# Normalised rows transposed by 32x32 blocks on VectorE and brought into channel order through DRAM

## The chip, the cores and the metric

The kernel runs on one core of a Trainium2 chip. The metric is device time in microseconds (us) of one execution, and lower is better. In the text PE is TensorE, DVE is VectorE, ACT is ScalarE, POOL is GpSimd and SP is SyncE, which issues every DMA of this kernel.

## What is computed

The input has 16 sequences of 1024 rows of 256 channels in float32. Each row is layer-normalised, and the normalised row feeds two branches whose results are added to the input:

```python
xn = _layernorm(x, axis=-1)
x = x + _L0_attn_ref(xn, Wqkv, Wout) + _L0_ffn_ref(xn, W1, b1, W2, b2)
# attention: 16 heads of 16 channels, segments of 512 rows; the keys and values are every 8th row of the segment
scores = jnp.einsum('bhspd,bhskd->bhspk', q4, k4)       # 512 queries x 64 keys in each segment and head
c = jnp.max(scores, axis=4, keepdims=True)              # over blocks of 64 queries
w = jnp.exp(scores - c)
out = jnp.einsum('bhsnmk,bhskd->bhsnmd', w, v4) / (jnp.sum(w, axis=-1) + 1e-10)[..., None]
# feed-forward: relu(xn @ W1 + b1) @ W2 + b2, 256 -> 1024 -> 256
```

## The kernel before

The work is cut into 32 segments of 512 rows. A segment's rows lie on 128 partitions, four rows to a partition. The five engines each run their own program, written out by hand, and meet only at semaphores, so the order on each engine is the order of the code. Matrix products are made with float32r operands in three parts: a tensor is split into a high part (a cast, on ACT) and a low part (the difference, on DVE or POOL), and `three_products` (L736 to L742) issues high x high, low x high and high x low.

A step `s` works on three segments at once: the feed-forward and the output product of segment `s` (`ffn`), the attention of segment `s+1` (`attention`), and the projections of segment `s+2` (`norm`), while segment `s+3` is loaded (`load`). All four are on in most steps. `par` is `s % 2`. The keys and values of two segments are projected together, in the steps with `par == 0`, called even steps here; the others are odd steps. A step has eight tiles of the feed-forward: `first_product` makes 128 hidden channels for 512 rows in `h_bank`, `hidden` (ACT) applies ReLU and makes the high part, `hidden_lo` (POOL) the low part, and `second_product` adds into `y_bank`.

What the change touches:

- DVE normalises segment `s+2` early in step `s` (`normalise`, four instructions, `xn` at L622), after the second of the eight `shift_scores`. In an even step `keys_lo` (`xkey_lo`, L598) follows it.
- PE transposes `xn` with eight 128x128 products against an identity into the two PSUM banks `misc` (`transpose_x`, L809), just ahead of the last `first_product` of the step.
- ACT waits for that last `first_product`, since it was still reading the same half of `xt`, and then copies the banks to `xt_hi` (`transposed_hi`, L487). DVE makes `xt_lo` (`transposed_lo`, L651).
- PE makes the queries of segment `s+2` from `xt` (`queries`, the products with `wq`) after `second_product` of tile 6 and the last `scores`.
- SP starts a step with `rden_to_dram`, waits for the two conditions of `load_x`, issues `rden_spread` (reciprocals of the softmax sums, copied to the rows that need them), and then for most of the step `pack`: 24 DMAs that bring keys and queries of pairs of heads to the partitions of the score product. Its last DMA is the output of the step before, `out<-y`.

The order of the eight transposes among the waits of PE is this (L801 to L810):

```python
pe.wait_ge(xn_ready, s + 3)
pe.wait_ge(num_den_ready, past((s + 1) * QUADS))
...
for c in range(DH):
    for t in range(T):
        mm = pe.transpose(misc[c][:, t * P:(t + 1) * P], xn[:, t, c * P:(c + 1) * P], identity[:])
    mm.then_inc(xt_psum, 1)
```

Of the kernel before, what the change touches and what calls it, by code (L numbers as in the profile page):

```python
# [28 lines left out]
P = 128  # L29
# [19 lines left out]
def ln_attention_ffn(nc, x, wq_t, wkv_t, wout_t, w1, b1, w2, b2, out):  # L49
# [18 lines left out]
    with ExitStack() as ctx:  # L68
# [28 lines left out]
        xn = sb("xn", [P, T, D], F32)  # L97
        xn_keys = sb("xn_keys", [P, D], F32)
# [18 lines left out]
        att_part = [sb(f"att_{n}", [P, 2, QUADS, SEG], F32R) for n in ("hi", "lo")]  # L117
# [45 lines left out]
        xn_keys_ready = sem("xn_keys_ready")  # L163
        xkey_psum = sem("xkey_psum")
# [94 lines left out]

        block = ctx.enter_context(nc.Block())  # L260

        @block.sync
        def _(sp):
# [67 lines left out]

            def step(s, par, ffn, attention, norm, load):
                if ffn:
                    rden_to_dram(s)
                if load:

                    sp.wait_ge(x_b2_ready, s + 2)
                    sp.wait_ge(xn_ready, s + 2)
                    load_x(s + 3, 1 - par)
                if load and par == 1:  # L340
                    sp.wait_ge(xn_keys_ready, s + 3)
                    load_keys(s + 3)
# [22 lines left out]
        def _(pool):  # L365
# [32 lines left out]
            def attention_lo(s, quad, par):  # L398
                pool.wait_ge(att_ready, s * QUADS + quad + 1)
                pool.wait_ge(att_hi, s * QUADS + quad + 1)  # L400
                pool.tensor_tensor(att_part[1][:, par, quad], att[:, quad], f32(att_part[0][:, par, quad]),  # L401
# [38 lines left out]
        def _(act):  # L440
# [22 lines left out]
            def attention_hi(s, quad, par):  # L463
                act.wait_ge(att_ready, s * QUADS + quad + 1)
                act.wait_ge(y_psum, past((s - 1) * YB))
                act.copy(att_part[0][:, par, quad], att[:, quad]).then_inc(att_hi, 1)  # L466
# [15 lines left out]
            def transposed_hi(s, par):  # L482

                act.wait_ge(h_psum, past((s + 1) * NH))
                for c in range(DH):
                    act.wait_ge(xt_psum, (s + 2) * DH + c + 1)
                    act.copy(xt[0][:, par, c], misc[c][:]).then_inc(xt_hi, 1)  # L487
# [63 lines left out]
        def _(dve):  # L551
# [65 lines left out]
            def normalise(s, par):  # L617
                dve.wait_ge(stats_ready, s + 1)
                dve.wait_ge(rstd_ready, s + 1)
                dve.wait_ge(xt_psum, past(s * DH))  # L620
# [3 lines left out]
                op.then_inc(xn_ready, 1)  # L624

# [21 lines left out]
            def transposed_lo(s, par):  # L647

                for c in range(DH):
                    dve.wait_ge(xt_hi, (s + 2) * DH + c + 1)  # L650
                    dve.tensor_tensor(xt[1][:, par, c], misc[c][:], f32(xt[0][:, par, c]),  # L651
                                      ALU.subtract).then_inc(xt_lo, 1)
# [82 lines left out]
        def _(pe):  # L735
# [40 lines left out]
            def output_product(s, par):  # L776
                pe.wait_ge(att_hi, (s + 1) * QUADS)
                pe.wait_ge(att_lo, (s + 1) * QUADS)
                for t in range(T):
                    mm = three_products(y_bank[t // 2][:, (t % 2) * D:(t % 2 + 1) * D],  # L780
                                        [([a[:, par, m, t * P:(t + 1) * P] for a in att_part],
# [17 lines left out]
            def transpose_x(s, par):  # L799
# [3 lines left out]
                pe.wait_ge(num_den_ready, past((s + 1) * QUADS))  # L803
                if par == 0 and not (isinstance(s, int) and s == -2):
                    pe.wait_ge(kv_ready, s + 4)
                    pe.wait_ge(k_ready, s + 4)
# [45 lines left out]
            def weighted_values_waits(s, norm):  # L852
# [4 lines left out]
                if norm:  # L857
                    pe.wait_ge(xt_lo, (s + 3) * DH)
# [11 lines left out]
            def step(s, par, ffn, attention, norm, load):  # L870
# [4 lines left out]
                for i in range(LAG, NH):  # L875
# [6 lines left out]
                    if i == NH - 1 and norm:  # L882
# [16 lines left out]
                if attention:  # L899
                    weighted_values_waits(s, norm)  # L900
# [53 lines left out]
```

## Time and profile before

| | |
|---|---|
| median of 3 runs | 1131.28 us (1129.73 to 1131.32) |
| the profiled execution | 1129.96 us, of it a span of 1128.1 us from the first to the last instruction |
| TensorE clock granted, mean | 0.995 |
| busy | PE 97%, DVE 66%, ACT 58%, POOL 55% of the span |
| DMA | 130.57 MB, mean 116 GB/s, packets 45.2% of the time of 16 engines |

A time in the text such as 574.01 is microseconds from the start of the span. The two steps that are read are an even step (about 523.5 to 558.3 us) and the odd step behind it (about 558.3 to 591.5 us). A busy share says how much an engine had to do, not whether the end waited for it; the chain of waits says that. Issue-to-landing times of DMAs run from the start of the issue on SP to the arrival of the last byte.

### The profile page before, as it was taken

The numbers are of one execution on the slowest core, as the hardware profiler recorded it, in microseconds if no ns is written. First come the engines' busy times: TensorE is split into PE (matmuls) and PEld (weight loads), VectorE is DVE, ScalarE is ACT, GpSimd is POOL, SyncE is SP. The second block draws the span as 40 slices with busy tenths as digits, with TensorE's granted clock in tenths as the row PEclk, the third lists the DMA queues.
The fourth block names the chain that finished last, engine by engine and source line by source line (L and its number), as shares of the span: only waits on it lengthen the run. The fifth ranks groups of instructions, "written<-read, shape, count | busy, mean of one in ns | idle before, by whom it ended". The sixth has DMA issues, their size and how long they took to land.

```text
span 1128.1 us, 23167 instructions
## 1 busy us (share of the span) xinstructions
PE 1097.2 (97%) x7457; PEld 944.5 (84%) x7457; DVE 742.9 (66%) x1370; ACT 650.4 (58%) x1078; POOL 620.1 (55%) x488
## 2 busy tenths in 40 slices
PE   5799999999999999999999999999999999999997
PEld 3588988888988888988888988888988888888886
DVE  7787667657666667666667666667676667677540
ACT  4556556555656555555665556565565565555652
POOL 2435555555555555565565556466465565565464
PEclk9999999999999999999999999999999999999999
DMA  5444444344444444445344544444544353544421
GB/s 183 107 119 128 120 125 120 95 123 118 127 122 110 111 112 126 121 115 126 92 126 111 135 108 110 117 120 118 128 103 122 100 134 107 139 102 106 98 77 68
DMA packets 96139, 130.57 MB, mean 116 GB/s; under 512 B 25840, under 2 KB 54128, under 8 KB 96112
## 3 DMA queue, kind: packets, MB, share of 16 engines
q1 hardware_dynamic: 96112, 130.23, 45.2%
q8 instruction: 15, 0.25, 0.1%
q14 instruction: 12, 0.10, 0.0%
HBM read 39.98 MB, written 18.87 MB: 52 GB/s over the span
## 4 chain that ended last, share of the span: by engine, by line
PE 96%; DVE 1%; issue 1%; POOL 1%; SPq 0%; DMA 0%; POOLq 0%; ACT 0%; DVEq 0%
PE y_bank L740 40%; PE h_bank L740 40%; PE s_banks L796 5%; PE misc L866 3%; PE s_banks L866 2%; PE misc L809 2%; PE misc L740 2%; PE misc L834 0%; PE misc L817 0%; PE s_banks L740 0%; DVE w_exp L637 0%; DVE s_max L631 0%; DMA q_pack<-q_hi 0%; DVE xn_keys L592 0%; DVE w_lo L556 0%
## 5 line engine op out<-in xcount | busy, mean ns | idle before, releaser
L389 POOL TENSOR_TENSOR h_lo<-h_full,h_hi 128x512 fp32r<-128x512 f32 x256 | 336.9, 1318 | 454.5 <-ACT h_full L455 450.0
L740 PE MATMUL y_bank<-w_hi,h_hi 128*128 128x256 f32 x1024 | 290.1, 283 | 1.2 <-ACT w_exp L461 1.2
L740 PE MATMUL y_bank<-w_lo,h_hi 128*128 128x256 f32 x1024 | 289.9, 283 | 0.0
L740 PE MATMUL y_bank<-w_hi,h_lo 128*128 128x256 f32 x1024 | 289.5, 283 | 0.0
L461 ACT ACTIVATE w_exp<-w_exp 128x512 f32<-128x512 f32 x256 | 162.6, 636 | 213.7 <-DVE w_exp L637 213.7
L453 ACT ACTIVATE h_hi<-h_bank,b_cols 128x512 fp32r<-128x512 f32 x256 | 175.9, 687 | 122.5 <-PE h_bank L740 117.2
L631 DVE TENSOR_REDUCE s_max<-s_banks 128x8 f32<-128x512 f32 x256 | 175.4, 685 | 64.8 <-PE s_banks L796 63.0
L740 PE MATMUL h_bank<-xt_hi,w_hi 128*128 128x512 f32 x512 | 211.0, 412 | 1.4 <-DVE q_lo L660 1.4
L740 PEld LDWEIGHTS y_bank<-w_hi,h_hi 128*128 128x128 f32 x1024 | 195.1, 191 | 10.7 <-issue 1.4
L740 PEld LDWEIGHTS y_bank<-w_lo,h_hi 128*128 128x128 f32 x1024 | 195.4, 191 | 9.9
L740 PE MATMUL h_bank<-xt_lo,w_hi 128*128 128x512 f32 x512 | 202.4, 395 | 0.0
L740 PE MATMUL h_bank<-xt_hi,w_lo 128*128 128x512 f32 x512 | 201.8, 394 | 0.0
L740 PEld LDWEIGHTS y_bank<-w_hi,h_lo 128*128 128x128 f32 x1024 | 194.6, 190 | 0.0
L637 DVE TENSOR_TENSOR w_exp<-s_banks,s_max 128x512 f32<-128x512 f32 x256 | 177.1, 692 | 11.0
L455 ACT ACTIVATE h_full<-h_bank,b_cols 128x512 f32<-128x512 f32 x256 | 175.1, 684 | 0.0
L707 DVE TENSOR_TENSOR y<-y_bank,x_b 128x512 f32<-128x512 f32 x64 | 44.3, 692 | 146.2 <-PE y_bank L740 146.2
L740 PEld LDWEIGHTS h_bank<-xt_hi,w_hi 128*128 128x128 f32 x512 | 96.6, 189 | 44.1 <-issue 27.8
L740 PEld LDWEIGHTS h_bank<-xt_hi,w_lo 128*128 128x128 f32 x512 | 96.5, 189 | 22.8
L740 PEld LDWEIGHTS h_bank<-xt_lo,w_hi 128*128 128x128 f32 x512 | 97.1, 190 | 14.9
L796 PE MATMUL s_banks<-q_pack,k_pack 96*128 96x512 f32 x256 | 97.3, 401 | 6.5 <-issue 2.3
L651 DVE TENSOR_TENSOR xt_lo<-misc,xt_hi 128x512 fp32r<-128x512 f32 x64 | 41.3, 686 | 86.5 <-ACT xt_hi L487 86.5
L401 POOL TENSOR_TENSOR att_lo<-att,att_hi 128x512 fp32r<-128x512 f32 x64 | 80.9, 1287 | 27.5 <-ACT att_hi L466 27.5
(90 smaller groups left out, 1601.0 us busy)
## 6 DMA issues: line engine op xcount, KB each, us to landing
q_pack<-q_hi SPq DMA_DIRECT2D x256, 128.0 KB, 2.4
x_raw<-x SPq DMA_DIRECT2D x32, 512.0 KB, 3.4
q_pack<-q_lo SPq DMA_DIRECT2D x128, 128.0 KB, 2.4
rden_rows<-rden_dram SPq DMA_DIRECT2D x128, 128.0 KB, 3.5
out<-y SPq DMA_DIRECT2D x32, 512.0 KB, 2.9
k_pack<-k_hi SPq DMA_DIRECT2D x256, 32.0 KB, 1.9
num_den<-num_den SPq DMA_DIRECT2D x32, 256.0 KB, 2.5
k_pack<-k_lo SPq DMA_DIRECT2D x128, 32.0 KB, 1.9
```

The source lines that it names most:

```text
L389: pool.tensor_tensor(h_part[1][:, i % HBUF], h_full[:, i % HBUF], f32(h_part[0][:, i % HBUF]), ALU.subtract).then_inc(h_lo, 1)
L401: pool.tensor_tensor(att_part[1][:, par, quad], att[:, quad], f32(att_part[0][:, par, quad]), ALU.subtract).then_inc(att_lo, 1)
L453: act.activation(h_part[0][:, i % HBUF], h_bank[i % 2][:], ACT.Relu, bias=b1_cols[:, i:i + 1]).then_inc(h_hi, 1)
L455: act.activation(h_full[:, i % HBUF], h_bank[i % 2][:], ACT.Relu, bias=b1_cols[:, i:i + 1]).then_inc(h_ready, 1)
L461: act.activation(w_exp[:, pair], w_exp[:, pair], ACT.Exp).then_inc(w_ready, 1)
L631: dve.tensor_reduce(s_max[:, pair], ps.rearrange("p t n i -> p n t i"), AX.XY, ALU.max).then_inc(max_ready, 1)
L637: dve.tensor_tensor(w_exp[:, pair].rearrange("p (t n i) -> p t n i", t=T, n=NB), ps, top, ALU.subtract).then_inc(s_shifted, 1)
L651: dve.tensor_tensor(xt[1][:, par, c], misc[c][:], f32(xt[0][:, par, c]), ALU.subtract).then_inc(xt_lo, 1)
L707: dve.tensor_tensor(y[:, par, 2 * b:2 * b + 2], y_bank[b][:].rearrange("p (t d) -> p t d", t=2), x_b2[:, par, 2 * b:2 * b + 2], ALU.add).t ...
L740: mm = pe.matmul(ps, stationary[a], moving[b], start=start and c == 0 and n == 0, stop=stop and c == len(pairs) - 1 and n == 2, skip_group ...
L796: pe.matmul(s_bank[n % 2], k_pack[0:PR, pair], q_pack[0:PR, pair], start=True, stop=True).then_inc(s_psum, 1)
L866: mm = pe.matmul(pv_banks[quad][PW * j:PW * (j + 1), a], v[rows, 1 - par, pair], w_exp[rows, pair], start=True, stop=True)
```

## The change

In the steps that have both `ffn` and `norm` (s = 0 to 29, thirty steps), PE no longer transposes `xn`. DVE transposes its 32x32 blocks into a new buffer `z` with one instruction behind `normalise`. SP writes `z` to DRAM in four DMAs, one for each group of 32 partitions, and reads it back in one DMA into `xt_raw`, whose partitions are channels. ACT and DVE make `xt_hi` and `xt_lo` from `xt_raw` in SBUF instead of `misc` in PSUM, with access patterns that put the rows in token order. The first two steps (s = -2 and -1) keep the transposes on PE. Waits on `misc` move accordingly. The attention rows `att_hi` and `att_lo` have one buffer instead of two, and `attention_hi` waits for the output product of the step before (`y_psum` at `s * YB`, it was `(s - 1) * YB`).

```diff
+        z = sb("z", [P, D // PW, T, PW], F32)
+        xt_raw = sb("xt_raw", [P, DH, SEG], F32)
+        xt_dram = nc.dram_tensor("xt_dram", [D // PW, PW, P // PW, P], F32).ap()
...
-        att_part = [sb(f"att_{n}", [P, 2, QUADS, SEG], F32R) for n in ("hi", "lo")]
+        att_part = [sb(f"att_{n}", [P, QUADS, SEG], F32R) for n in ("hi", "lo")]
...
+        def block_order(tile):
+            return tile.rearrange("p (i t n) -> p t i n", i=P // PW, t=T)
+
+        def token_order(tile):
+            return tile.rearrange("p (t i n) -> p t i n", i=P // PW, t=T)
...
+            def blocks_to_dram(s):
+
+                sp.wait_ge(z_ready, s + 1)
+                for i in range(P // PW):
+                    sp.dma_start(xt_dram[:, :, i].rearrange("j c n -> c j n"),
+                                 z[PW * i:PW * (i + 1)].rearrange("c j t n -> c j (t n)")).then_inc(xt_out, 16)
+
+            def transposed_in(s):
+
+                sp.wait_ge(xt_out, (s + 1) * 64)
+                sp.dma_start(xt_raw[:], xt_dram.rearrange("(a j) c i n -> (j c) a (i n)", a=DH)).then_inc(xt_in, 16)
+
             def step(s, par, ffn, attention, norm, load):
+                if ffn and norm:
+                    blocks_to_dram(s)
                 if ffn:
                     rden_to_dram(s)
+                if ffn and norm:
+                    transposed_in(s)
                 if load:
...
             def attention_hi(s, quad, par):
                 act.wait_ge(att_ready, s * QUADS + quad + 1)
-                act.wait_ge(y_psum, past((s - 1) * YB))
+                act.wait_ge(y_psum, past(s * YB))
...
             def transposed_hi(s, par):
 
                 act.wait_ge(h_psum, past((s + 1) * NH))
+                if not (isinstance(s, int) and s < 0):
+                    act.wait_ge(xt_in, (s + 1) * 16)
                 for c in range(DH):
...
+                        act.copy(token_order(xt[0][:, par, c]), block_order(xt_raw[:, c])).then_inc(xt_hi, 1)
...
+            def transpose_blocks(s):
+
+                dve.wait_ge(xn_ready, s + 3)
+                dve.transpose(z[:].rearrange("p j t n -> p t j n"),
+                              xn[:].rearrange("p t (j n) -> p t j n", n=PW)).then_inc(z_ready, 1)
...
+                        dve.tensor_tensor(token_order(xt[1][:, par, c]), block_order(xt_raw[:, c]),
+                                          token_order(f32(xt[0][:, par, c])), ALU.subtract).then_inc(xt_lo, 1)
...
                     if n == 1 and norm:
                         normalise(s + 2, par)
+                    if n == 1 and norm and ffn:
+                        transpose_blocks(s)
                     if n == 1 and keys:
                         keys_lo(s)
...
-                    if i == NH - 1 and norm:
+                    if i == NH - 1 and norm and not ffn:
                         transpose_x(s, par)
```

On PE, between the second product of tile 5 and the last first product of a step, the rows before were these (`L801` and `L755` rows set a register for a wait):

```order
L740 MATMUL y_bank<-w_lo,h_hi 128x256
L740 MATMUL y_bank<-w_hi,h_lo 128x256
L801 REGISTER_ALU
L809 MATMUL misc<-identity,xn 128x128 x8
L755 REGISTER_ALU
L740 MATMUL h_bank<-xt_hi,w_hi 128x512
L740 MATMUL h_bank<-xt_lo,w_hi 128x512
```

and now they are these:

```order
L788 MATMUL y_bank<-w_lo,h_hi 128x256
L788 MATMUL y_bank<-w_hi,h_lo 128x256
L803 REGISTER_ALU
L788 MATMUL h_bank<-xt_hi,w_hi 128x512
L788 MATMUL h_bank<-xt_lo,w_hi 128x512
```

The eight transposes are gone from PE, and nothing stands in their place.

On SP, at the turn from an even to an odd step of the changed program's first steps, the rows before were these:

```order
L303 DMA q_pack<-q_hi 32x2x512
L358 DMA out<-y 128x1024
L322 DMA rden_dram<-rden 128x64
L265 DMA x_raw<-x 128x1024
L269 DMA x_keys<-x 128x256
L328 DMA rden_rows<-rden_dram 32x1x1024 x4
L296 DMA k_pack<-k_hi 32x2x128 x2
```

and now they are these:

```order
L315 DMA q_pack<-q_hi 32x2x512
L386 DMA out<-y 128x1024
L348 DMA xt_dram<-z 32x8x128 x4
L334 DMA rden_dram<-rden 128x64
L354 DMA xt_raw<-xt_dram 128x2x512
L277 DMA x_raw<-x 128x1024
L281 DMA x_keys<-x 128x256
L340 DMA rden_rows<-rden_dram 32x1x1024 x4
L308 DMA k_pack<-k_hi 32x2x128 x2
```

Four writes stand between the output of the step before and the reciprocals, and one read between the reciprocals and the load of the next segment.

On DVE, behind the second `shift_scores` of a step, the rows before were these:

```order
L637 TENSOR_TENSOR w_exp<-s_banks,s_max 128x512
L622 TENSOR_SCALAR xn<-x_raw,mean_var,rstd 128x256 x4
L631 TENSOR_REDUCE s_max<-s_banks 128x8
L637 TENSOR_TENSOR w_exp<-s_banks,s_max 128x512
L631 TENSOR_REDUCE s_max<-s_banks 128x8
```

and now they are these:

```order
L679 TENSOR_TENSOR w_exp<-s_banks,s_max 128x512
L658 TENSOR_SCALAR xn<-x_raw,mean_var,rstd 128x256 x4
L665 STREAM_TRANSPOSE z<-xn 128x4x8x32
L673 TENSOR_REDUCE s_max<-s_banks 128x8
L679 TENSOR_TENSOR w_exp<-s_banks,s_max 128x512
```

One instruction over 1024 elements per partition is added; in an even step `xkey_lo` comes right behind it.

## Rows read from the trace of the kernel before

**Rows 1.** The page, busy time and share of each engine, and granted clock in 40 slices

```profile
PE 1097.2 (97%) x7457; PEld 944.5 (84%) x7457; DVE 742.9 (66%) x1370; ACT 650.4 (58%) x1078; POOL 620.1 (55%) x488
...
PEclk9999999999999999999999999999999999999999
```

**Rows 2.** Chain of waits in order of time, odd step: start us, us, what

```profile
574.01 0.87 PE misc L809 x8
574.89 1.40 PE h_bank L740 x6
```

**Rows 3.** The same chain in the even step

```profile
540.93 0.87 PE misc L809 x8
```

**Rows 4.** Timeline of ACT, DVE and PE: start, us, engine, line; both steps

```profile
576.40 1.07 ACT L487 CAST xt_hi<-misc 128x512 fp32r<-128x512 f32 x2 [2.77 <-PE h_bank L740]
...
577.02 1.29 DVE L651 TENSOR_TENSOR xt_lo<-misc,xt_hi 128x512 fp32r<-128x512 f32 x2 [2.99 <-ACT xt_hi L487]
...
579.46 0.40 PE L740 MATMUL h_bank<-xt_hi,wq_hi 128*128 128x512 f32 x1
...
543.30 1.07 ACT L487 CAST xt_hi<-misc 128x512 fp32r<-128x512 f32 x2 [2.74 <-PE h_bank L740]
...
546.38 0.40 PE L740 MATMUL h_bank<-xt_hi,wq_hi 128*128 128x512 f32 x1
```

**Rows 5.** Timeline of SP's queue at the start of the even and the odd step

```profile
533.60 0.42 SPq L358 DMA_DIRECT2D out<-y  x1
538.48 0.32 SPq L322 DMA_DIRECT2D rden_dram<-rden  x1
539.14 0.35 SPq L265 DMA_DIRECT2D x_raw<-x  x1
...
566.97 0.60 SPq L303 DMA_DIRECT2D q_pack<-q_lo  x1
567.61 0.60 SPq L303 DMA_DIRECT2D q_pack<-q_hi  x1
568.52 0.36 SPq L358 DMA_DIRECT2D out<-y  x1
...
572.60 0.32 SPq L322 DMA_DIRECT2D rden_dram<-rden  x1
573.30 0.34 SPq L265 DMA_DIRECT2D x_raw<-x  x1
```

**Rows 6.** DMA issues: copy, count, KB each, median us from issue to landing

```profile
q_pack<-q_lo SPq DMA_DIRECT2D x128, 128.0 KB, 2.4
...
rden_dram<-rden SPq DMA_DIRECT2D x32, 32.0 KB, 1.4
y<-wkv_t SPq DMA_DIRECT2D x1, 512.0 KB, 5.1
```

**Rows 7.** Landing times of the tiles x_raw and rden_rows, us

```profile
DMA to landing us min/median/max: 3.1/3.4/7.3
...
DMA to landing us min/median/max: 2.5/3.5/4.3
```

**Rows 8.** Groups of instructions by form: count, busy us, mean ns

```profile
L556 DVE TENSOR_TENSOR wkv_lo<-y,wkv_hi 128x1024 fp32r<-128x1024 f32 x1 | 1.2, 1222 | 0.0
```

**Rows 9.** Timeline of DVE and POOL around the normalisation, even step, then odd

```profile
530.51 2.46 POOL L410 TENSOR_TENSOR x_b<-x_raw,b_rows 128x1024 f32<-128x1024 f32 x1
...
530.62 0.41 DVE L598 TENSOR_TENSOR xkey_lo<-misc,xkey_hi 128x256 fp32r<-128x256 f32 x1
...
533.08 0.40 PE L740 MATMUL misc<-wkv_hi,xkey_hi 128*128 128x512 f32 x1
...
561.82 2.36 DVE L622 TENSOR_SCALAR xn<-x_raw,mean_var,rstd 128x256 f32<-128x256 f32 x4
...
562.55 1.47 POOL L389 TENSOR_TENSOR h_lo<-h_full,h_hi 128x512 fp32r<-128x512 f32 x1 [2.83 <-ACT h_full L455]
563.98 2.45 POOL L410 TENSOR_TENSOR x_b<-x_raw,b_rows 128x1024 f32<-128x1024 f32 x1
```

More of the change, by code:

```diff
@@ L163, in ln_attention_ffn @@
         xn_keys_ready = sem("xn_keys_ready")
+        z_ready = sem("z_ready")
+        xt_out = sem("xt_out")
+        xt_in = sem("xt_in")
         xkey_psum = sem("xkey_psum")
@@ L400, in attention_lo @@
                 pool.wait_ge(att_hi, s * QUADS + quad + 1)
-                pool.tensor_tensor(att_part[1][:, par, quad], att[:, quad], f32(att_part[0][:, par, quad]),
+                pool.tensor_tensor(att_part[1][:, quad], att[:, quad], f32(att_part[0][:, quad]),
                                    ALU.subtract).then_inc(att_lo, 1)
@@ L464, in attention_hi @@
                 act.wait_ge(att_ready, s * QUADS + quad + 1)
-                act.wait_ge(y_psum, past((s - 1) * YB))
-                act.copy(att_part[0][:, par, quad], att[:, quad]).then_inc(att_hi, 1)
+                act.wait_ge(y_psum, past(s * YB))
+                act.copy(att_part[0][:, quad], att[:, quad]).then_inc(att_hi, 1)
             def attention_drain(s, quad):
@@ L484, in transposed_hi @@
                 act.wait_ge(h_psum, past((s + 1) * NH))
+                if not (isinstance(s, int) and s < 0):
+                    act.wait_ge(xt_in, (s + 1) * 16)
                 for c in range(DH):
-                    act.wait_ge(xt_psum, (s + 2) * DH + c + 1)
-                    act.copy(xt[0][:, par, c], misc[c][:]).then_inc(xt_hi, 1)
+                    if isinstance(s, int) and s < 0:
+                        act.wait_ge(xt_psum, (s + 2) * DH + c + 1)
+                        act.copy(xt[0][:, par, c], misc[c][:]).then_inc(xt_hi, 1)
+                    else:
+                        act.copy(token_order(xt[0][:, par, c]), block_order(xt_raw[:, c])).then_inc(xt_hi, 1)
             def queries_hi(s, m):
@@ L619, in normalise @@
                 dve.wait_ge(rstd_ready, s + 1)
-                dve.wait_ge(xt_psum, past(s * DH))
+                if isinstance(s, int) and s <= 2:
+                    dve.wait_ge(xt_psum, s * DH)
+                else:
+                    dve.wait_ge(z_ready, s - 2)
                 for t in range(T):
@@ L650, in transposed_lo @@
                     dve.wait_ge(xt_hi, (s + 2) * DH + c + 1)
-                    dve.tensor_tensor(xt[1][:, par, c], misc[c][:], f32(xt[0][:, par, c]),
-                                      ALU.subtract).then_inc(xt_lo, 1)
+                    if isinstance(s, int) and s < 0:
+                        dve.tensor_tensor(xt[1][:, par, c], misc[c][:], f32(xt[0][:, par, c]),
+                                          ALU.subtract).then_inc(xt_lo, 1)
+                    else:
+                        dve.tensor_tensor(token_order(xt[1][:, par, c]), block_order(xt_raw[:, c]),
+                                          token_order(f32(xt[0][:, par, c])), ALU.subtract).then_inc(xt_lo, 1)
             def finish_projections(s, par):
@@ L780, in output_product @@
                     mm = three_products(y_bank[t // 2][:, (t % 2) * D:(t % 2 + 1) * D],
-                                        [([a[:, par, m, t * P:(t + 1) * P] for a in att_part],
+                                        [([a[:, m, t * P:(t + 1) * P] for a in att_part],
                                           [w[:, m, :] for w in wout]) for m in range(DH)],
@@ L801, in transpose_x @@
                 pe.wait_ge(xn_ready, s + 3)
[L803 to L806, printed above, removed]
                 for c in range(DH):
@@ L850, in queries, with weighted_values_waits @@
                                True, True).then_inc(q_psum, 1)
-            def weighted_values_waits(s, norm):
+            def weighted_values_waits(s, par, norm):
                 pe.wait_ge(v_ready, (s + 2) * 2)
                 pe.wait_ge(w_ready, (s + 2) * PAIRS)
-                if norm:
-                    pe.wait_ge(xt_lo, (s + 3) * DH)
+                if norm and isinstance(s, int) and s == -1:
+                    pe.wait_ge(xt_lo, 2 * DH)
+                elif norm and par == 0:
+                    pe.wait_ge(k_ready, s + 4)
             def weighted_values(s, quad, par):
@@ L899, in step @@
                 if attention:
-                    weighted_values_waits(s, norm)
+                    weighted_values_waits(s, par, norm)
                 if ffn:
```

## The prediction, on record before the changed kernel ran

> **What bounds the kernel now.** I read the page first: PE is busy for 97% of the span and its granted clock stays in the top tenth in every slice; DVE, the next, is at 66% [rows 1]. The reader is to see an engine that never rests, beside others with room. Busy time alone proves nothing, so I read the chain of waits next. In both steps it lies on PE all through the transposes, and eight of them stand on it with 0.87 us each time [rows 2, 3]. They finish right where the last first product begins (574.01 + 0.87 = 574.88), so there is no wait around them to fill the gap if they go. Then I read the timeline around the place where the transposed rows are used, and SP's queue, because the new path runs through it.
>
> **The change, part by part.**
>
> *Removed from PE.* Eight transposes in each of thirty steps, on the chain: 30 x 0.87 = 26.1 us. This is the whole gain that is there to be had: 1129.96 - 26.1 = 1103.9 us in the profiled execution.
>
> *When the rows are needed.* ACT starts `xt_hi` when the last first product is through, at 576.40 in the odd step and 543.30 in the even one [rows 4]. Without the transposes both moments come 0.87 us sooner: 575.53 and 542.43. From that start to the end of `xt_lo` it takes 577.02 + 1.29 - 576.40 = 1.91 us [rows 4]. PE wants the result for the queries at 579.46 and 546.38 [rows 4], now at 578.59 and 545.51. So `xt_raw` may land as late as 1.91 us, and some 0.1 us for two semaphores, before these: 576.6 in the odd step, 543.5 in the even.
>
> *The new path through SP.* SP must first finish the packing of the step before. Its last DMA, `out<-y`, starts at 533.60 and 568.52 and takes 0.42 and 0.36 us [rows 5]; then come the four writes of `z`. No row shows such a write. Its issue is nearest to `q_pack`'s, also 32 partitions in several runs, one every 0.64 us [rows 5]. In the odd step they start at 568.95, 569.59, 570.23 and 570.87, in the even one the last starts at 535.98. A write of 128 KB is nearest in size to `q_pack` with 2.4 us from issue to landing; below lies the small write to DRAM, `rden_dram`, with 1.4 [rows 6], above `rden_rows` with up to 4.3 [rows 7]. I take 2.4: the last lands at 573.27 and 538.38. SP meanwhile waits for the reciprocals, whose copy it issues at 572.60 and 538.48 as before, since DVE makes them behind scores that PE sets the time of. So the read goes out at 573.3 in the odd step and 539.1 in the even one, which are the times of `x_raw` before [rows 5].
>
> *The read.* It is 512 KB from DRAM over 128 partitions. `x_raw` has the same size in longer runs: 3.1 at best, median 3.4 us [rows 7]. `wkv_t` has this very form, but was loaded at the start beside other loads: 5.1 us [rows 6]. In the steady steps nothing is in flight ahead of the read but `z`, which it waits for, so I take 3.4: landed at 576.7 and 542.5. The odd step is then late by 576.7 - 576.6 = 0.1 us, and the even one has 1.0 us to spare. Sum: 15 x 0.87 + 15 x (0.87 - 0.1) = 24.6 us.
>
> *Added to DVE.* One block transpose over 1024 elements. No row shows one; the nearest DVE instruction over 1024 elements from and to SBUF takes 1.22 us [rows 8]. A shorter one would change nothing in the sum; upwards no row gives a bound, and I allow twice that, 2.4 us. It delays `xkey_lo`, which ran from 530.62 to 531.03, while its product starts on PE at 533.08 [rows 9]. With 1.22 us it ends at 532.25: hidden. With 2.4 us it ends at 533.43 and costs 0.4 us in 15 even steps, 6 us. The shifts of scores behind it move by the same time, and DVE waits for PE a little later, so they catch up. In the odd step there is no `xkey_lo`. `z` itself is ready near 532 and 565.4, long before SP is free, so DVE's time is not on the new path.
>
> *Moved on SP.* Five DMAs stand ahead of `x_raw` and `rden_rows`. `rden_rows` then lands about 1 us later, and POOL's `att`, `att_hi` and `att_lo` with it; the output product that needs them comes last in the step, behind two tail products of 3 us together, so I cost this at nothing. If that cover were gone, it would cost at most the 1 us, 30 us in all.
>
> *Costed at nothing:* the copies from SBUF instead of PSUM (they are in the 1.91 us; if each of the four took 0.1 us more, 15 odd steps lose 3 us); the single buffer of attention rows (`attention_hi` runs after the queries of its step, the product it now waits for ended a whole step earlier); the waits on `misc`.
>
> *The sum* is 1129.96 - 24.6 = 1105.4 us. The profiled execution is 1.3 us below the median of the runs, so the median should be near 1107.
>
> **The rivals.**
>
> *The round trip through DRAM is longer than its row (ends slower).* Place: the read's landing, ahead of ACT's `xt_hi`. What speaks for it: margins of -0.1 and 1.0 us against two transfers for which there is no row of their own, one behind the other, and an SP queue that is full from `q_lo` to `out<-y`. If queries are late, so are `q_lo`, the next packing and the next writes: nothing is made up. An excess e on the read costs e in the odd step and e - 1.0 in the even one. It decides at 0.1 + e + e - 1.0 = 1.74, that is e = 1.3 us: beyond that the kernel is slower. At the 5.1 us of `wkv_t` e is 1.7: an odd step gains 0.87 - 1.8 = -0.93, an even one 0.87 - 0.7 = 0.17, and 15 pairs lose 11 us: 1143. If the write takes 4.3 us instead, the odd step is 2.0 late and the even one 0.2: loss 0.46 per pair, 1138. Against it: `x_raw`, as large and at the same moment of the step, has a median of 3.4 [rows 7].
>
> *The block transpose waits for POOL.* DVE's fourth `xn` of each step does: four of them take 2.36 us where POOL's `h_lo` runs through their end, 562.55 + 1.47 = 564.02, and they end at 564.18 [rows 9]. POOL's `x_b` comes right behind, until 532.97 in the even step and 566.43 in the odd [rows 9]. If the transpose waits for that, it ends at 534.19 and 567.65. In the even step `xkey_lo` then ends at 534.6 and its product is 1.57 us late: 15 x 1.57 = 23.6 us. In the odd step three shifts of 1.4 us follow, the reciprocals come 1.0 us later, and the read 0.65 us: 10 us. Together 1107 + 34 = 1141. Against it: `xkey_lo`, 0.41 us from 530.62 on, runs beside `x_b` without such a wait [rows 9]. The Trainium skill, "SBUF — State Buffer", in its terms and its account of the engine side, says that DVE and GpSimd share a pair of ports under an exclusive lock, held for a whole instruction, when DVE runs in a two-port mode. By that rule, and if the transpose is such an instruction, this rival's 1141 us comes out; if it reads through one port, my sum stands. The trace agrees with the lock for `xn` and cannot show it for the transpose.
>
> *Part of the gain is eaten.* Excesses of 0.5 to 1.2 us on the new path, or a transpose of 2.4 us: 15 x 0.5 = 8 to 15 x 1.2 + 15 x 0.2 = 21 us less, so 1115 to 1128.
>
> **How the numbers follow.** The forecast (1104 to 1114) has 0.48; the gain partly eaten (1114 to 1129) 0.22; the longer round trip (1129 to 1150) 0.18; the transpose behind POOL (1130 to 1142) 0.10; something I do not see, at either side, 0.02. Predicted is the likeliest, 1107 us. The range reaches from the full gain, with a little below for the runs' spread, to 1136, which takes in about half of the two slow cases. A measurement of this kernel can tell about 0.2%, 2.3 us, from no change. Faster by more than that needs under 1129: 0.70; within it 0.05; slower 0.25.
>
> **What would show each step right or wrong.** The transposes on PE fall from 256 to 16 and the chain no longer names them in the steady steps. The block transpose shows 1.2 us, and 2.4 or more if I am wrong. The wait of ACT's `xt_hi` names the DMA `xt_raw` in the odd steps, for about 1 us, and PE waits for `xt_lo` by 0.1 us there and not at all in the even steps. Landing times: 2.4 us for `z`, 3.4 for `xt_raw`. The span of an odd step falls by more than 0.7 us, of an even step by 0.87. What would make the prediction wrong: PE idle ahead of the queries by a microsecond or more in every odd step, or ahead of the keys' product in every even step.

## The result, and the profile of the changed kernel

The changed kernel takes 1137.86 us (median of 4 runs, 1136.87 to 1138.81), the kernel before on the same chip 1131.3 us. The ratio is 1.005 with a 95% interval from 1.0032 to 1.0068: slower by about 0.6%, where 2.1% faster was forecast. The profiled execution has a span of 1135.1 us at a mean granted clock of 0.988, against 1128.1 us and 0.995.

The page of the changed kernel, with busy times, the granted clock in 40 slices, and the chain of waits by engine:

```profile
PE 1082.4 (95%) x7217; PEld 924.0 (81%) x7217; DVE 781.8 (69%) x1400; ACT 648.9 (57%) x1078; POOL 619.7 (55%) x488
...
PEclk9879999999999999999999999999999999999999
...
PE 75%; SPq 10%; DMA 5%; issue 4%; ACT 2%; DVE 2%; POOL 1%; POOLq 0%; ACTq 0%; DVEq 0%
```

PE has 240 fewer matmul records and is busy for 14.8 us less, and the span is still 7.0 us longer. SP's queue and DMAs now stand on the chain. The waits say where (us in total, times, longest):

```profile
ACT xt_hi L520 <- DMA xt_raw<-xt_dram: 98.7, 30, 5.2
...
PEld h_bank L788 <- ACT xt_hi L520: 25.1, 16, 4.8
PE h_bank L788 <- ACT xt_hi L520: 18.0, 13, 4.5
```

Sixteen times PE's weight loads wait for the transposed rows: in the fifteen odd steps and in step 0. In the timeline of SP, ACT and DVE in an odd step the path can be followed from copy to copy (start us, us, engine, line):

```profile
508.11 0.37 SPq L386 DMA_DIRECT2D out<-y  x1
508.54 2.77 SPq L348 DMA_DIRECT2D xt_dram<-z  x4
512.08 0.34 SPq L334 DMA_DIRECT2D rden_dram<-rden  x1
513.42 0.38 SPq L354 DMA_DIRECT2D xt_raw<-xt_dram  x1
...
517.04 1.14 ACT L520 CAST xt_hi<-xt_raw 128x512 fp32r<-128x512 f32 x2 [3.93 <-DMA xt_raw<-xt_dram]
...
517.69 1.29 DVE L697 TENSOR_TENSOR xt_lo<-xt_raw,xt_hi 128x512 fp32r<-128x512 f32 x2 [4.20 <-ACT xt_hi L520]
```

These answer to [rows 4, 5]. `xt_lo` ends at 518.98, and the chain shows PE idle until then in the odd step ("issue"), and in the even step behind it without a pause:

```profile
517.99 0.24 PE s_banks L844
518.23 0.86 issue
519.09 3.01 PE h_bank L788 x12
...
553.10 0.23 PE s_banks L844
553.33 2.74 PE h_bank L788 x12
```

The page's DMA issues (count, KB each, us from issue to landing) answer to [rows 6, 7]. The copies that stand behind the new ones land later too: `x_raw` takes 4.7 (3.4 before), `rden_rows` 4.5 (3.5).

```profile
xt_dram<-z SPq DMA_DIRECT2D x120, 128.0 KB, 3.0
xt_raw<-xt_dram SPq DMA_DIRECT2D x30, 512.0 KB, 3.6
```

The block transpose, which no row of before showed, stands in the timeline of DVE and POOL like this:

```profile
503.45 2.45 POOL L438 TENSOR_TENSOR x_b<-x_raw,b_rows 128x1024 f32<-128x1024 f32 x1
...
503.68 1.25 DVE L665 STREAM_TRANSPOSE z<-xn 128x1024 f32<-128x1024 f32 x1
```

**Step by step.** I took the first query product of each step from the trace and the distances between them. The steady steps are those that end with the queries of steps 4 to 27, twelve even and twelve odd. The table has the distances in us, and the difference of the two kernels:

| | before | after | difference |
|---|---|---|---|
| queries of step 3 begin at | 172.01 | 182.21 | +10.2 |
| steady even step | 34.83 | 34.06 | -0.77, twelve times -9.2 |
| steady odd step, mean | 33.07 | 33.38 (33.14 to 33.75) | +0.30, twelve times +3.6 |
| steps 28 and 29 together | 68.14 | 68.91 | +0.8 |
| from there to PE's end | 69.24 | 70.84 | +1.6 |

The sum is +7.0 us, which is the difference of the spans. So the steady steps gain 5.6 us, where 24.6 were forecast for all thirty and 19.7 of them for these twenty-four, and the first steps lose nearly twice as much as the steady ones gain.

**The first step.** The chain at the end of step 0:

```profile
69.53 0.56 DVE rden L687
70.09 0.02 issue
70.11 0.34 SPq L334
70.44 0.04 issue
70.49 4.65 DMA xt_raw<-xt_dram
75.13 0.02 issue
75.15 0.02 ACTq L514
75.17 0.04 issue
75.21 1.15 ACT xt_hi L520 x2
76.36 0.90 issue
77.26 5.46 PE h_bank L788 x12
```

Step 0 has no output of an earlier step and is short, so DVE's reciprocals are late within it. The read stands behind their copy in SP's queue and waits for them, although the four writes were issued by 66.6 us and had landed by 68.6. PE is idle for 4.5 us, and then twelve products take 5.46 us that take 3.01 in the odd step above. The busy times by stretches (us, then PE, PEld, DVE, ACT and POOL, granted clock, DMA share, GB/s) show why:

```profile
72.00:76.00 4.00, 0.75 (x6) 0.42 (x4) 0.15 (x2) 0.79 (x2) 0.00 (x0) 1.00 0.84 305
76.00:80.00 4.00, 2.74 (x7) 2.19 (x8) 3.93 (x7) 1.97 (x5) 0.70 (x1) 0.51 0.41 88
80.00:84.00 4.00, 4.00 (x19) 3.42 (x17) 2.19 (x4) 2.19 (x5) 2.01 (x3) 0.64 0.12 25
```

After the idle stretch the granted clock is 0.51 and 0.64 of the full 2.4 GHz, that is the lower level of 1.2 GHz all through the first and for most of the second.

A part of the difference lies ahead of the first step that the change touches. In step -1 both kernels wait 0.74 us for the first query product; then the twelve products take 4.45 us in the changed kernel and 3.00 in the one before. The same kind of row, first the changed kernel, then the one before:

```profile
40.00:44.00 4.00, 2.50 (x6) 1.68 (x6) 3.93 (x7) 2.27 (x6) 0.00 (x0) 0.74 0.18 67
```

```profile
40.00:44.00 4.00, 2.69 (x11) 2.01 (x12) 3.93 (x7) 2.27 (x5) 0.00 (x0) 1.00 0.14 52
```

So the table's +10.2 us is what these two executions show, and not all of it is the new path's.

### The profile page after: what moved, and what is told of

Its sections match the earlier page's. It is cut to its first block, busy times and chain, and to the rows that moved or that the text cites. A ratio compares the mean times of both kernels' runs of the same rounds, so it can differ in the third digit from the quotient of the medians.

```text
span 1135.1 us, 22820 instructions
## 1 busy us (share of the span) xinstructions
PE 1082.4 (95%) x7217; PEld 924.0 (81%) x7217; DVE 781.8 (69%) x1400; ACT 648.9 (57%) x1078; POOL 619.7 (55%) x488
## 4 chain that ended last, share of the span: by engine, by line
PE 75%; SPq 10%; DMA 5%; issue 4%; ACT 2%; DVE 2%; POOL 1%; POOLq 0%; ACTq 0%; DVEq 0%
PE h_bank L788 33%; PE y_bank L788 31%; PE s_banks L844 4%; SPq L308 3%; DMA xt_raw<-xt_dram 3%; SPq L315 3%; PE misc L912 3%; PE s_banks L912 2%; DMA xt_dram<-z 2%; PE misc L788 2%; SPq L348 1%; SPq L322 1%; ACT xt_hi L520 1%; ACT h_full L483 1%; ACT num_den L501 1%
## 5 line engine op out<-in xcount | busy, mean ns | idle before, releaser
L755 DVE TENSOR_TENSOR y<-y_bank,x_b 128x512 f32<-128x512 f32 x64 | 44.2, 691 | 131.9 <-PE y_bank L788 131.9
L697 DVE TENSOR_TENSOR xt_lo<-xt_raw,xt_hi 128x512 fp32r<-128x512 f32 x60 | 38.8, 688 | 105.8 <-ACT xt_hi L520 105.8
L424 POOL TENSOR_TENSOR att<-num_den,rden_rows 128x512 f32<-128x512 f32 x64 | 85.1, 1351 | 38.3 <-DMA rden_rows<-rden_dram 38.3
```

The lines of the kernel that those rows point to most:

```text
L424: pool.tensor_tensor(att[:, quad], num_den[:, quad, 0], rden_rows[:, quad], ALU.mult).then_inc(att_ready, 1)
L697: dve.tensor_tensor(token_order(xt[1][:, par, c]), block_order(xt_raw[:, c]), token_order(f32(xt[0][:, par, c])), ALU.subtract).then_inc(x ...
L755: dve.tensor_tensor(y[:, par, 2 * b:2 * b + 2], y_bank[b][:].rearrange("p (t d) -> p t d", t=2), x_b2[:, par, 2 * b:2 * b + 2], ALU.add).t ...
```

## The experiments

Each is compared with the kernel before on its own chip, which took 1132.4 to 1132.5 us there (median); the changed kernel ran where that took 1131.3, so a difference between its median and one of these is uncertain by about 1 us. "Queries of step 3" and "steady steps" are meant as in the table above.

**Rows of the step before.** The new path keeps all its work, but ACT and DVE split the rows that were read a step earlier, so no read is ever late. The projections are therefore made from another segment's rows. The read has moved behind the second packing too, and it takes two DRAM tensors in turn.

```diff
-                if ffn and norm:
-                    transposed_in(s)
                 if load:
...
                     pack(s, 1)
+                if ffn and norm:
+                    transposed_in(s, par)
...
-                    act.wait_ge(xt_in, (s + 1) * 16)
+                    act.wait_ge(xt_in, past(s * 16))
```

> The changed kernel, but ACT and DVE split in each step the rows that the read of the step before brought, and the read is issued behind the second packing instead of ahead of the load (it computes the projections from the rows of another segment; all work, copies and DMAs are kept). Theory L (the rows land too late: write of z, then read, one behind the other on SP): the waits of xt_hi for the read are gone, PE has no gap ahead of the queries in any step, and the transposes' 0.78 us of an even step come in odd steps too and in the first steps: 1131.3 - 30 x 0.78 = 1108 us, between 1105 and 1112. Rival C (the added DVE instruction, the copies from SBUF and 1 MB more of DMA per step slow the other work): the time stays near 1138, at least above 1128. Rival F (only the first steps lose): they are repaired here too, the odd steps keep 0.25 us of loss: about 1126.

Measured: 1109.24 us, ratio 0.979 (0.978 to 0.981). Steady steps are 34.02 and 32.20 us, 0.82 and 0.87 less than before, and the queries of step 3 begin at 170.51. This is the gain that was forecast, and it comes when the moment of landing is taken out.

**The first two steps on PE.** Steps 0 and 1 keep the eight transposes; one fill of `z` with zeros ahead of the steps keeps the count of its semaphore.

```diff
+    FIRST = 2
...
+        def by_dram(s):
+            return not (isinstance(s, int) and s < FIRST)
...
-                if ffn and norm:
+                if ffn and norm and by_dram(s):
                     blocks_to_dram(s)
...
-                    if i == NH - 1 and norm and not ffn:
+                    if i == NH - 1 and norm and not (ffn and by_dram(s)):
                         transpose_x(s, par)
```

> The changed kernel, with steps 0 and 1 transposed by PE as before; the new path starts at step 2. Theory L with its second part (the loss is in two places: 9.9 us in steps 0 to 3, where a step is short and PE's clock falls behind a wait of 4.5 us, and about 1 us of late rows in each odd step of the rest, which takes back more than the 0.87): the time falls by about 10 to 12 us to 1126 to 1128, and PE's gaps of 0.8 to 1.4 us in odd steps stay. Rival F (the first steps are the whole loss): odd steps would show no gap, 1108. Rival C (a cost spread over all steps): 1136 or more.

Measured: 1129.41 us (10 runs), ratio 0.998 (0.997 to 0.999). The queries of step 3 begin at 173.55 instead of 182.21, the steady odd steps are 33.27. The queries come 8.7 us sooner, so most of the early loss comes in with the first two steps on the new path. Not all of the 8.7 is the edit's: the query products of step -1, ahead of all that it touches, already end 1.9 us sooner here. The time is 1.4 us above what was expected, and steps 28 and 29 take 70.15 us, 1.2 more than in the changed kernel; why, no run shows.

**The writes from ACT's queue.** ACT issues the four writes ahead of the third exponential, SP the read ahead of the reciprocals' copy.

```diff
-                if ffn and norm:
-                    blocks_to_dram(s)
+                if ffn and norm:
+                    transposed_in(s)
                 if ffn:
                     rden_to_dram(s)
-                if ffn and norm:
-                    transposed_in(s)
...
+                    if i == 4 and ffn and norm:
+                        blocks_to_dram(s)
```

> The changed kernel, with the four writes of z issued by ACT ahead of its third exponential, about 3 us sooner than SP can, and the read ahead of the reciprocals on SP. Theory L: z has landed when SP comes to the read, so the rows land some 2 to 3 us sooner, all gaps ahead of the queries go, in the first steps too: 1108 us, 1105 to 1114. If ACT's issue of four DMAs takes 2.5 us as on SP, h_hi and w_exp of the third tile come 1 us later, which their cover holds. Rival C: no better than 1128. Rival R (the reciprocals behind the read make the attention rows late for the output product): gaps ahead of the products with wout.

Measured: 1116.27 us, ratio 0.986 (0.984 to 0.988). Steady steps are 34.02 and 32.21, as with the rows of the step before, and step 3's queries begin at 171.85. In the waits PE's products name the transposed rows once instead of thirteen times (its weight loads once instead of sixteen):

```profile
ACT xt_hi L518 <- DMA xt_raw<-xt_dram: 64.4, 28, 3.3
...
PE h_bank L788 <- ACT xt_hi L518: 1.7, 1, 1.7
```

The time is 2 us above the expected range. The steady steps are as expected; the 4.9 us by which the span is longer than with the rows of the step before lie at the ends: 1.3 us by the queries of step 3, 2.0 in steps 28 and 29, 1.4 behind them.

**The path unused.** The kernel before, with the single buffer of attention rows, the block transpose, the four writes and the read added; nothing uses their result, and PE still transposes. Here the block transpose also waits for the read of the step before, a wait that the changed kernel does not have.

```diff
+                if ffn and norm:
+                    blocks_to_dram(s)
                 if ffn:
                     rden_to_dram(s)
+                if ffn and norm:
+                    transposed_in(s)
...
-                act.wait_ge(y_psum, past((s - 1) * YB))
+                act.wait_ge(y_psum, past(s * YB))
```

> The kernel before with one buffer of attention rows, and with the block transpose, the four writes and the read added at their new places, their result unused; PE transposes as before and ACT and DVE split from PSUM. Theory L: what is added costs nothing by itself, 1131 to 1133 us. Rival C (the added instruction and DMAs slow the rest): 1138 or more, with no gap ahead of the queries but longer steps.

Measured: 1138.85 us, ratio 1.006 (1.004 to 1.008). The steady steps are 34.83 and 33.07, to 0.01 us those of before: there everything that the change adds is free. That is the time of rival C, but not its reason, since the steady steps are no longer. Step 3's queries begin 4.6 us later, steps 28 and 29 take 1.4 us more, and from there to the end it is 1.5 us more. The chain in step 0:

```profile
77.80 2.53 POOL att L418 x2
...
82.93 4.60 PE y_bank L771 x24
```

The attention rows there wait for `rden_rows`, whose copies stand behind the new ones, and the output product waits for them for 1.83 us. Its 24 products take 4.60 us, 3.04 in the kernel before, at a granted clock of 0.89 and then 0.68. The wait and the slower products are 3.4 of the 4.6 us.

**The writes ahead of the output.** On SP the four writes go ahead of the last DMA of a step, the 512 KB of `out<-y`.

```diff
             def step(s, par, ffn, attention, norm, load):
-                if ffn and norm:
-                    blocks_to_dram(s)
...
                     pack(s, 3)
+                if load and not (isinstance(s, int) and s < -1):
+                    blocks_to_dram(s + 1)
                 if ffn:
```

> The changed kernel with the four writes of z ahead of the store out<-y on SP, 0.43 us sooner. Theory L (in an odd step the chain from SP's last packing over write and read to the queries sets the time): an odd step's gap ahead of the queries falls from about 0.9 us by 0.4 us, even steps stay, so 14 x 0.4 = 6 us less than the changed kernel, 1132 us. A rival by which the read waits for something else (the reciprocals) changes nothing: 1138.

Measured: 1123.96 us, ratio 0.992 (0.990 to 0.994): 13.9 us below the changed kernel, where 6 were expected. The steady odd steps are 32.63. SP's timeline in an odd step:

```profile
501.88 0.60 SPq L315 DMA_DIRECT2D q_pack<-q_hi  x1
502.52 2.15 SPq L348 DMA_DIRECT2D xt_dram<-z  x4
504.95 0.38 SPq L386 DMA_DIRECT2D out<-y  x1
506.73 0.34 SPq L334 DMA_DIRECT2D rden_dram<-rden  x1
507.19 0.39 SPq L354 DMA_DIRECT2D xt_raw<-xt_dram  x1
```

The four issues take 2.15 us instead of 2.77, and a write lands in 2.5 us (median of all 120) instead of 3.0. But the read waits for the last of the four. That one now has the store right behind it and takes 2.97 us in the mean of the steady odd steps, 2.82 behind the store. From the first issue to the last landing these steps need 4.64 us instead of 4.86. So a steady odd step, 0.74 us shorter, owes only 0.2 us to faster writes. Most of it, 0.67 us, is their earlier start: 0.43 for the store's place and 0.24 in which SP waited for `y` ahead of the store, which the expected 0.4 left out. The read gives back 0.1 (3.86 instead of 3.75). Twelve such steps are 8.9 us; the queries of step 3 come 2.8 us sooner.

The Trainium skill, "DMA: Bandwidth & Descriptors", under its queues and completion order, says that a DMA's semaphore is raised only after every earlier write of the same DMA engine; by that rule a landing shown here contains what is left of the store ahead of it. The first three writes agree with it: 3.19, 3.36 and 2.84 us behind the store, 2.35, 2.52 and 2.42 ahead of it. The last one, slow with the store behind it, is not accounted for by it, and no run here shows the rule engine by engine.

**A fifth write.** One more DMA of 128 KB from `z` to a spare tensor ahead of the four, and the read waits for it as well.

```diff
+                sp.dma_start(spare, z[0:PW].rearrange("c j t n -> c j (t n)")).then_inc(xt_out, 16)
...
-                sp.wait_ge(xt_out, (s + 1) * 64)
+                sp.wait_ge(xt_out, (s + 1) * 80)
```

> The changed kernel with a fifth write of 128 KB of z, to a spare DRAM tensor, ahead of the four; nothing reads it but the read waits for it too. Theory L: the four writes and the read come 0.65 to 0.7 us later, each odd step is longer by that, even steps still have 0.8 us to spare and stay: 15 x 0.7 = 10 us more, 1148. A rival by which the loss does not hang on SP's issue times: 1138 to 1140.

Measured: 1152.01 us, ratio 1.019 (1.016 to 1.021). The steady odd steps are 34.12, 0.75 more than with four writes. Of the even ones eleven are 34.05 to 34.14, as with four writes, and one, step 4, is 35.73. Once the odd step is late it pays for a DMA in full, while the even step's slack of some 0.8 us takes all of it in eleven of twelve steps. The time is 4 us above what was expected; step 4 (1.7 us), steps 28 and 29 (1.4) and the first steps (0.9) make that up.

**The keys first, and the residual later.** The kernel with the writes from ACT, the block transpose behind `xkey_lo`, and POOL's residual `x_b` two tiles later.

```diff
-                    if n == 1 and norm and ffn:
-                        transpose_blocks(s)
                     if n == 1 and keys:
                         keys_lo(s)
+                    if n == 1 and norm and ffn:
+                        transpose_blocks(s)
...
-                    if i == 2 and attention:
+                    if i == 4 and attention:
                         residual(s, par)
```

> The kernel with the writes from ACT, and two moves: the block transpose behind xkey_lo on DVE, and POOL's residual sum x_b two tiles later, so that the fourth xn does not have to wait for both of POOL's instructions. Theory L and the lock: the gaps of 1.2 us at the keys' product and at first products, where the four xn take 4.5 us, are gone, and PE has no gap in the steady steps: 1116 - 3 to 5 = 1112 us, 1108 to 1114. If POOL's later residual delays h_lo for the second products, or the load of x, gaps appear there: 1116 or more.

Measured: 1110.68 us (5 runs), ratio 0.981 (0.979 to 0.982): the best complete version. Steps 28 and 29 take 66.22 us, 1.9 less than before.

**The residual alone**, in the kernel before.

```diff
-                    if i == 2 and attention:
+                    if i == 4 and attention:
                         residual(s, par)
```

> The kernel before with only POOL's residual sum x_b two tiles later. PE never waited for xn there, so no change: 1130 to 1133 us. If it is faster by more than 2 us, part of what the combined version gains does not come from the change.

Measured: 1129.95 us (10 runs), ratio 0.998 (0.997 to 0.999). So about 2 us of the version above have nothing to do with the change.

**The keys first alone**, with the writes from ACT.

```diff
-                    if n == 1 and norm and ffn:
-                        transpose_blocks(s)
                     if n == 1 and keys:
                         keys_lo(s)
+                    if n == 1 and norm and ffn:
+                        transpose_blocks(s)
```

> The kernel with the writes from ACT, and the block transpose behind the keys' low part in even steps. The residual stays where it was. If the order of these two is what exposes the keys' product in step 28 (1.24 us of idle PE), and the residual's place the rest of what the version with both edits gained, this kernel loses that gap: 1116.3 - 1.3 = 1115 us, and the remaining 4 us to 1110.7 are the residual's and shorter first steps. If the transpose's place alone brings everything, it gives 1111 us. If the order costs nothing, 1116 us.

Measured: 1117.16 us, ratio 0.986 (0.983 to 0.989), not to be told from 1116.27. The gap ahead of the keys' product in step 28 is gone, but gaps of 0.9 to 1.2 us stand ahead of first products in steps 1, 28 and 29. Inconclusive in time: the edit moves a stall of one step, and what else the residual's place does beside it stays open.

**The read ahead of the reciprocals.** The changed kernel with these two calls on SP in the other order.

```diff
-                if ffn:
-                    rden_to_dram(s)
                 if ffn and norm:
                     transposed_in(s)
+                if ffn:
+                    rden_to_dram(s)
```

> The changed kernel, with the read of the transposed rows ahead of the copy of the reciprocals on SP. Theory (in the short step 0 the read stands behind a copy that waits for DVE until 70.11 us, while the blocks have landed near 68.6): the gap ahead of the queries of step 0 falls from 4.5 us by about 1.5 us and its low granted clock is shorter, so the first steps cost 7 instead of 10 us; in the steady odd steps the read is bound by the blocks' landing and stays, but the reciprocals go out 1.3 us later, behind it: nothing on PE. In all 1135 us. Rival (the first steps' cost is the filled queue and the read's own 4.7 us): no change there, 1138 us. Second rival: the later reciprocals hold up the attention rows and the output product in each step, and it gets slower than 1138 us.

Measured: 1129.31 us (10 runs), ratio 0.998 (0.997 to 0.9995), 8.5 us below the changed kernel. The step 3 queries begin at 175.18, 7.0 us sooner. Its chain at the end of step 0:

```profile
67.69 3.81 DMA xt_raw<-xt_dram
...
71.57 1.15 ACT xt_hi L520 x2
72.72 0.90 issue
73.62 3.00 PE h_bank L788 x12
```

The read goes out 2.8 us sooner, its landing takes 3.81 us instead of 4.65, PE's gap is 3.2 us instead of 4.5, and the twelve products run in 3.00 us instead of 5.46. The steady odd steps gain 0.21 us as well, to 33.16, which none of the theories had: the read lands in 3.59 us there instead of 3.75, and the last write 0.06 sooner.

The gain of the whole kernel is plain: its slowest run, 1133.74 us, lies below the fastest of the changed kernel, 1136.87. How it divides within the first steps is not shown by these two profiles, since they differ before the first of the swapped calls. The query products of step -1 take 2.97 us here, 4.45 there; SP comes to the writes 0.8 us sooner, and DVE has the reciprocals 2.3 us sooner. Of the read's 2.8 us the order explains at most the 1.9 between the blocks' landing at 68.56 and the read at 70.49. And in the kernel with the writes ahead of the output, whose step 0 has the changed kernel's order, the read lands in 3.60 us and the products take 4.50: two executions of one order differ by a microsecond in each.

**Three orders on SP and DVE at once**: the writes ahead of the output, the read ahead of the reciprocals, the keys first. Of these the first:

```diff
                     pack(s, 3)
+                if load and not (isinstance(s, int) and s < -1):
+                    blocks_to_dram(s + 1)
                 if ffn:
```

The other two are as above.

> Three orders at once, all on SP and DVE: the four writes ahead of the output of the step before, the read ahead of the copy of the reciprocals, and the block transpose behind the keys' low part. If the gains are separate: 1124.0 (the writes ahead alone) - 1.3 (step 28) - about 2.5 (first step) = 1120 us. If the first step's loss is the filled queue, 1123 us. If the writes from SP are bound to end behind those from ACT by the packing ahead of them, it stays above the 1110.7 us of that version, by 5 to 12 us.

Measured: 1116.74 us, ratio 0.987 (0.984 to 0.989). The steady odd steps are 32.27. That is 3 us below the 1120 us that separate gains would give, and 6 us above the best version, as the third case had it. Orders on SP and DVE give the same as a second queue for the writes.

## Why the prediction was wrong

**Where the forecast and the measurement part.** The forecast took 24.6 us off the span, and the changed kernel added 7.0: 31.6 us between them. Of these 14.1 lie in the twenty-four steady steps (19.7 forecast, 5.6 gained), 13.5 in the first steps (3.3 forecast, 10.2 lost), 2.4 in steps 28 and 29, and 1.6 behind them.

**What held.** PE's transposes are worth what they take on the chain: 0.82 and 0.87 us a steady step, where landing is not late. The block transpose takes 1.25 us, 1.22 was taken, and runs beside POOL's `x_b` without waiting for it, so the rival of the shared ports fell; by the lock that the Trainium skill describes ("SBUF — State Buffer", the engine side), the transpose is not an instruction that takes it, since it runs from 503.68 to 504.93 inside the 503.45 to 505.90 of `x_b`. The SBUF copies cost nothing (1.94 us from `xt_hi` to `xt_lo`'s end, 1.91 before), nor does the single buffer in the steady steps (path unused). The even step kept its slack.

**What failed first: "The odd step is then late by 0.1 us".** It was late by 1.0 us in the step shown (33.23 from query to query, 32.20 without lateness) and by 1.2 in the mean. From `out<-y` to the queries 519.09 - 508.11 = 10.98 us pass, and my working had 579.46 - 0.87 + 0.1 - 568.52 = 10.17. The 0.81 are made up of three terms:
- *the writes*: the read goes out 5.31 us behind the start of `out<-y`, 4.78 were taken: 0.53. The last of the four is issued 2.45 us behind that start instead of 2.35, and it lands in 2.84 us instead of the 2.4 that I had taken from `q_pack`. That `q_pack` has no 512 KB store next to it and these have is the likeliest reason: in step 0, without a store, the last write lands in 2.52, and with the store behind it instead of ahead it still takes 2.97 in the mean.
- *the read*: 3.6 us instead of 3.4: 0.2. In four of the twelve steady odd steps it is 3.8 to 4.1, which makes most of the spread up to 33.75.
- *the hand-offs* to ACT, DVE and PE: the rest, under 0.1.

With the 0.1 of the forecast that makes 0.9; the remaining 0.1 is `out<-y` itself, 22.25 us behind the queries of the step before, 22.14 in the kernel before. The rival of the longer round trip had the right place. By its own rule an excess e costs an odd step e and an even one nothing up to 1.0 us, and with e about 1.1 in the mean the steady steps keep a small gain, which they do: 5.6 us.

**What failed second: thirty steps were counted as one pattern.** The sum took step 0 like step 15, and it alone has a late copy of the reciprocals ahead of the read. It was this term, of the wrong sign, that turned a small gain into a loss: the first steps cost 10.2 us where 3.3 of gain were in the sum. The two steps on PE and the swap of two calls bring most of it back (the queries of step 3 come 8.7 and 7.0 us sooner), so the new path in step 0, the queue's order in it and the low clock behind the wait are shown as the main cause. The exact shares are not: at the queries of step -1, which the change doesn't touch, the changed kernel's profile is already 1.45 us behind by its clock alone. The new copies ahead of `rden_rows` cost the unused path 4.6 us, with PE's transposes still there; in the changed kernel PE never waits for the output product of step 0, whose rows are ready by then, so that sum can't be added to this one.

**What failed third: "The output product comes last, so I cost this at nothing", and the hidden `xkey_lo`.** Both hold in the steady steps. The first fails only in the kernels whose queries of step 0 are not late: the output product of step 0 waits 1.83 us in the unused path and 0.85 with the rows of the step before, and not at all in the changed kernel. The second fails once in the changed kernel. In step 28 the four `xn` take 4.52 us instead of 2.35; they did so in the kernel before too, 4.53, and `xkey_lo` was just in time there. With the transpose between, `xkey_lo` ends at 1014.43, where its product would have begun at 1013.28:

```profile
1008.33 4.52 DVE L658 TENSOR_SCALAR xn<-x_raw,mean_var,rstd 128x256 f32<-128x256 f32 x4
1012.88 1.25 DVE L665 STREAM_TRANSPOSE z<-xn 128x1024 f32<-128x1024 f32 x1
1014.05 0.38 DVE L631 TENSOR_TENSOR xkey_lo<-misc,xkey_hi 128x256 fp32r<-128x256 f32 x1
```

It costs 1.26 us of idle PE, once.

**The last 1.6 us** can't be ascribed. 1.5 of them lie in the last output product (see below), with the same wait ahead of it in both kernels. The versions with the rows of the step before and with a fifth write have the whole path in them and run that product in 3.1 us, as the kernel before does. But the other nine of the eleven profiles with the path take 4.4 to 5.5, and the two without it 3.1, so that the change makes the slower case likelier is not excluded.

## What to carry to other kernels

A path that runs through a queue ends when the queue's order lets it: put the copy that the bound engine waits for ahead of those that nobody waits for yet, and ahead of one that itself waits for another engine. When a landing time is borrowed from another copy, look at what is in flight ahead of each of them; 0.5 us of it, fifteen times over, was a third of the forecast gain here. And work out the first and the last steps of a pipeline by themselves, since waits that are hidden in the middle come out there.

## What was not expected of the hardware

- The same four writes of 128 KB take 2.15 us to issue and 2.5 us to land (median), or 2.77 and 3.0 behind a store of 512 KB on the same queue. The one that is next to the store in front of it is slow too, 2.97 us in the mean.
- A gap of 4.5 us on PE is followed by a granted clock of 0.51 and 0.64 in the next two stretches of 4 us; after one of 3.2 us, in the kernel with the read ahead, twelve products run in 3.00 us. The gap alone does not decide it: with the writes from ACT and the keys first they take 4.58 us behind a gap of 1.95.
- The same idle time is not always answered alike. Ahead of the last output product PE is idle for 3.26 us in both kernels. In the kernel before the 24 products then take 3.12 us, in the changed one 4.61, at these granted clocks (first the changed kernel, then the one before):

```profile
1128.00:1130.00 2.00, 2.00 (x11) 2.00 (x11) 0.69 (x1) 0.00 (x0) 0.00 (x0) 0.50 0.00 0
```

```profile
1122.00:1124.00 2.00, 2.00 (x19) 2.00 (x18) 0.69 (x1) 0.00 (x0) 0.00 (x0) 1.00 0.00 0
```

Of the thirteen profiles four have 3.1 us here, eight 4.4 to 4.6 and one 5.5, all behind a wait of 3.25 or 3.26 us. Which an execution gets is not settled by these runs; 1.5 us of a comparison of two spans can be this alone.
